# Routing in plain fp32 in four column groups, choosing and placing once per batch

## The reference

```python
h = einsum('bsd,bdh->bsh', x, W[cat]) + b[cat][:, None, :]     # 4 x 1024 x 512
probs = softmax(h.reshape(4096, 512) @ Wr)                     # 4096 x 8
eidx = argmax(probs)                                           # first of the largest
rank = tokens of the same expert before this one               # keep if rank < 512
y[token] = p_tok * (relu(h[token] @ W1[eidx]) @ W2[eidx])      # 512 -> 2048 -> 512
out = x + y
```

## Time and profile before

| | |
|---|---|
| median of 3 runs | 889.83 us (889.78 to 892.02) |
| span of the profiled execution | 890.8 us, mean clock 0.978 |
| TensorE busy | 866.2 us (97%) |
| VectorE, ScalarE, GpSimd busy | 381.9, 253.8, 106.8 us |
| DMA | 126.85 MB, 142 GB/s on average |

### The profile page before, as it was taken

How to read it: one execution, slowest core, us unless ns; L and a number is a source line. 1 busy time by engine, 2 the same in 40 slices (tenths; PEclk the granted TensorE clock), 3 DMA queues, 4 the chain that set the end, 5 groups by cost and what they waited for, 6 DMA issues and landing times.

```text
span 890.8 us, 10524 instructions
## 1 busy us (share of the span) xinstructions
PE 866.2 (97%) x4072; PEld 702.9 (79%) x4073; DVE 381.9 (43%) x603; ACT 253.8 (28%) x361; POOL 106.8 (12%) x120
## 2 busy tenths in 40 slices
PE   8999998899999999999999999999999999999993
PEld 5777775688888888888888888888888888888882
DVE  4576665333343334333434343434343434343432
ACT  3322220323222322232223222322232223222320
POOL 1000001401030103010301030103010300040001
PEclk9898999899999999999999999999999999999997
DMA  8885773823343334233433352334233522241001
GB/s 294 297 296 188 252 281 144 277 98 109 128 168 115 111 126 175 108 114 122 169 107 115 120 179 104 120 116 179 104 118 118 179 100 94 94 170 60 0 0 47
DMA packets 52857, 126.85 MB, mean 142 GB/s; under 512 B 4409, under 2 KB 4409, under 8 KB 52195
## 3 DMA queue, kind: packets, MB, share of 16 engines
q1 hardware_dynamic: 42674, 93.35, 30.1%
q0 software_dynamic: 9584, 32.16, 9.9%
q10 hardware_dynamic: 576, 1.05, 0.4%
HBM read 110.13 MB, written 25.17 MB: 152 GB/s over the span
## 4 chain that ended last, share of the span: by engine, by line
PE 95%; DMA 2%; issue 0%; DVE 0%; SPq 0%; POOL 0%; ACT 0%; POOLq 0%; DVEq 0%
PE acc_ps L793 39%; PE y_ps L776 39%; PE acc_ps L720 7%; PE tp_ps L720 3%; PE y_ps L651 2%; PE tp_ps L666 2%; PE tp_ps L750 2%; DMA stage<-cond_w 1%; DMA h_rows<-rows 1%; DMA rows<-h_rows,tok_all 0%; PE y_ps L699 0%; PE y_ps L750 0%; PE y_ps L675 0%; POOL out L338 0%; PE acc_ps L729 0%
## 5 line engine op out<-in xcount | busy, mean ns | idle before, releaser
L776 PE MATMUL y_ps<-w_split,xt_split 128*128 128x512 f32 x1536 | 371.6, 392 | 0.0
L793 PE MATMUL acc_ps<-xt_split,w_split 128*128 128x512 f32 x1536 | 367.9, 389 | 1.1 <-issue 1.1
L793 PEld LDWEIGHTS acc_ps<-xt_split,w_split 128*128 128x128 f32 x1536 | 288.3, 188 | 61.1 <-issue 1.3
L776 PEld LDWEIGHTS y_ps<-w_split,xt_split 128*128 128x128 f32 x1536 | 286.0, 188 | 58.6
L615 DVE SCALAR_TENSOR_TENSOR xt_split<-acc_ps,xt_split 128x512 fp32r<-128x512 f32 x128 | 88.5, 692 | 386.2 <-ACT xt_split L434 375.7
L434 ACT ACTIVATE xt_split<-acc_ps 128x512 fp32r<-128x512 f32 x128 | 76.6, 598 | 494.0 <-PE acc_ps L793 474.2
L544 DVE TENSOR_TENSOR w_split<-stage,w_split 128x1024 fp32r<-128x1024 f32 x66 | 81.1, 1230 | 19.6 <-ACT w_split L385 18.1
L550 DVE TENSOR_TENSOR w_split<-stage,w_split 128x1024 fp32r<-128x1024 f32 x66 | 80.9, 1226 | 16.4 <-ACT w_split L391 16.4
L338 POOL DMA_INDIRECT out<-rows,put_all x32 | 31.7, 991 | 350.9 <-DVE rows L635 346.1
L720 PE MATMUL acc_ps<-w_split,xt_split 128*128 128x512 f32 x264 | 70.7, 422 | 1.7 <-DVE w_split L465 1.6
L385 ACT ACTIVATE w_split<-stage 128x1024 fp32r<-128x1024 f32 x66 | 69.4, 1051 | 0.0
(11 more groups left out here) (80 smaller groups left out, 261.7 us busy)
## 6 DMA issues: line engine op xcount, KB each, us to landing
stage<-w SPq DMA_DIRECT2D x64, 1024.0 KB, 5.3
stage<-x_t SPq DMA_DIRECT2D x7, 1024.0 KB, 7.3
h_rows<-rows POOLq DMA_DIRECT2D x7, 1024.0 KB, 7.5
stage<-cond_wt SPq DMA_DIRECT2D x4, 1024.0 KB
stage<-cond_w SPq DMA_DIRECT2D x3, 1024.0 KB
stage<-x_t ACTq DMA_DIRECT2D x4, 256.0 KB, 3.3
stage<-cond_w SPq DMA_DIRECT2D x4, 256.0 KB, 3.2
b_rows<-cond_b SPq DMA_DIRECT2D x4, 256.0 KB, 8.3
```

The lines of the kernel that those rows point to most:

```text
L776: last = nc.tensor.matmul(y_ps[:, s, :], hts[:, j % 2, a, s * P:(s + 1) * P], w2s[:, slot, w, kk, :], start=(j == 0 and (a, w) == (HI, HI) ...
L793: last = nc.tensor.matmul(acc_ps[:, j % 2, :], w1s[:, slot, w, k, jj * P:(jj + 1) * P], xts[:, par, a, k, :], start=(k == 0 and (w, a) == ...
```

## The change

- The logits are made in plain fp32 and from the raw x chunk in `stage`, not from its split. The four blocks of the contraction don't add up in one place: block k writes the 32 partitions 32k to 32k+31 of `turn_ps`, with a weight of 32 columns of which eight hold numbers. The sum over the four comes with the turn to tokens: `by_token` is a matmul of the copied logits with `fold`, a 128x8 matrix of four 8x8 identities.
- The product of matrix and Wr is made in the same two steps: `m_turn` (four fp32 matmuls with 512 moving columns, and four of one column for the bias), ScalarE's `copy_turned`, and `m_sum` (four fp32 matmuls with eight columns). VectorE's `copy_m` copies it without a split.
- choose, exps, rank_of, place and fill_table run once for a batch, over eight token tiles.
- The splits of x are two instructions of two blocks each, but for chunk 0.
- SyncE's loads wait for the route that reads the raw chunk (`s_lt`) beside its split, and for `s_turn` in the place of `s_m`.
- The lists of tiles are new. ScalarE's order within a tile is split_xt, split_cond, copy_turned, copy_logits, exps; TensorE's is cond_tile, fill_table, m_turn, m_sum, route, by_token, rank_of.

```diff
-    ROUTE = [3, 5, 7, 9] + [TPC * (c - 1) for c in range(4, NCH)]
-    CHOOSE = [n + 1 for n in ROUTE]
-    PLACE = [n + 2 for n in ROUTE]
-    FILL = [n + 4 for n in ROUTE]
-    PRODUCT = [ROUTE[CPB * b] - (2 if b > 1 else 1) for b in range(BATCH)]
-
-    SPLIT_X = [None, (1, 1, 2, 2), (4, 4, 5, 5), (6, 6, 7, 7)] + [range(TPC * (c - 2), TPC * (c - 1)) for c in range(4, NCH)]
-    SPLIT_W = [None, (4, 5, 6, 6)] + [tuple(2 * TPC * (b - 1) + n for n in (1, 3, 3, 4)) for b in range(2, BATCH)]
+    TPB = TPC * CPB
+    G = 32
+
+    M_TURN = [1, 7, 13, 19]
+    M_SUM = [2, 8, 14, 20]
+    ROUTE = [3, 4, 9, 10, 15, 17, 22, 24]
+    CHOOSE = [5, 11, 18, 25]
+    PLACE = [6, 13, 20, 27]
+    FILL = [8, 15, 22, 29]
+
+    SPLIT_X = [None, (1, 2), (5, 6), (7, 8), (11, 13), (12, 14), (17, 18), (19, 21)]
+    SPLIT_W = [None, (4, 5, 6, 6)] + [tuple(2 * TPC * (b - 1) + n for n in (1, 3, 3, 5)) for b in range(2, BATCH)]
...
             for b in range(1, BATCH):
-                sp.wait_ge(s_xlo, DK * (CPB * b - 1))
+                sp.wait_ge(s_xlo, 2 * (CPB * b - 1) + DK - 2)
+                sp.wait_ge(s_lt, CPB * b - 1)
                 load_xt(CPB * b)
                 sp.wait_ge(s_wlo, DK * b)
                 sp.dma_start(stage[:, 1, :, :], cond_view(b)).then_inc(s_stage[1], 16)
-                sp.wait_ge(s_m, b)
+                sp.wait_ge(s_turn, b)
                 load_cond_wt(b)
-                sp.wait_ge(s_xlo, DK * CPB * b)
+                sp.wait_ge(s_xlo, 2 * CPB * b + DK - 2)
+                sp.wait_ge(s_lt, CPB * b)
                 load_xt(CPB * b + 1)
                 load_bias_rows(b)
                 copy_x(b)
...
+            def copy_turned(b):
+                act.wait_ge(s_turn, b + 1)
+                if b >= 1:
+                    act.wait_ge(s_lg, b)
+                nc.scalar.activation(logits_t[:, 1, :], turn_ps, ACTF.Copy).then_inc(s_turnc, 1)
+
             def copy_logits(c):
-                act.wait_ge(s_msplit, c // CPB + 1)
+                act.wait_ge(s_mcopy, c // CPB + 1)
                 act.wait_ge(s_lt, c + 1)
-                if c >= 2:
-                    act.wait_ge(s_lg, c - 1)
-                nc.scalar.activation(logits_t[:, c % 2, :], tp_ps[0:16, 0, :], ACTF.Identity,
-                                     bias=bias16[:, (c // CPB) % 2:(c // CPB) % 2 + 1]).then_inc(s_ltc, 1)
+                nc.scalar.activation(logits_t[:, c % 2, :], turn_ps, ACTF.Identity,
+                                     bias=bias_g[:, (c // CPB) % 2:(c // CPB) % 2 + 1]).then_inc(s_ltc, 1)
...
+            then(nc.vector.memset(fold[:, :], 0.0))
+            dve.wait_ge(s_mask, 12)
+            for g in range(DK):
+                last = nc.vector.tensor_copy(fold[g * G:g * G + E, :], ident[g * G:g * G + E, g * G:g * G + E])
+            last.then_inc(s_fold, 1)
...
-            def m_product(b):
+            def m_turn(b):
 
                 pe.wait_ge(s_stage[0], 16 * (b + 1))
                 if b == 0:
                     pe.wait_ge(s_const, 16 * (BATCH + 1))
+                    pe.wait_ge(s_wr0, 2)
                 else:
-                    pe.wait_ge(s_msplit, b)
+                    pe.wait_ge(s_ltc, CPB * b)
+                    pe.wait_ge(s_mcopy, b)
+                for k in range(DK):
+                    nc.tensor.matmul(turn_ps[k * G:(k + 1) * G, :], wr32[:, k, :], stage[:, 0, k, :],
+                                     start=True, stop=True)
+                for k in range(DK):
+                    last = nc.tensor.matmul(bias_ps[k * G:(k + 1) * G, :], wr32[:, k, :], b_col[:, b, k:k + 1],
+                                            start=True, stop=True)
+                last.then_inc(s_turn, 1)
+
+            def m_sum(b):
+
+                pe.wait_ge(s_turnc, b + 1)
+                if b == 0:
+                    pe.wait_ge(s_fold, 1)
                 for m in range(DK):
-                    for k in range(DK):
-                        nc.tensor.matmul(m_ps[:, m, :], stage[:, 0, k, m * P:(m + 1) * P], wr16[:, k, 0:E],
-                                         start=(k == 0), stop=(k == DK - 1))
-                for k in range(DK):
-                    last = nc.tensor.matmul(bias_ps, wr16[:, k, :], b_col[:, b, k:k + 1],
-                                            start=(k == 0), stop=(k == DK - 1))
+                    last = nc.tensor.matmul(m_ps[:, m, :], logits_t[:, 1, m * P:(m + 1) * P], fold[:, :],
+                                            start=True, stop=True)
                 last.then_inc(s_m, 1)
 
             def route(c):
 
-                pe.wait_ge(s_msplit, c // CPB + 1)
-                pe.wait_ge(s_xlo, DK * (c + 1))
+                pe.wait_ge(s_mcopy, c // CPB + 1)
                 if c >= 1:
+                    pe.wait_ge(s_stage[2 + c % 2], 16 * ((c + 1) // 2))
+                if c % CPB:
                     pe.wait_ge(s_ltc, c)
                 for k in range(DK):
-                    for part in (HI, LO):
-                        last = nc.tensor.matmul(tp_ps[0:16, 0, :], m_split[:, k, :], xts[:, c % 4, part, k, :],
-                                                start=(k == 0 and part == HI), stop=(k == DK - 1 and part == LO))
+                    last = nc.tensor.matmul(turn_ps[k * G:(k + 1) * G, :], m32[:, (c // CPB) % 2, k, :],
+                                            stage[:, 2 + c % 2, k, :], start=True, stop=True)
                 last.then_inc(s_lt, 1)
 
-            def by_token(c):
+            def by_token(b):
...
+                for t in range(TPB):
+                    last = nc.tensor.matmul(tok_ps[:, t, :], logits_t[:, t // TPC, (t % TPC) * P:(t % TPC + 1) * P],
+                                            fold[:, :], start=True, stop=True)
                 last.then_inc(s_lg, 1)
```

More of the change, by code:

```diff
@@ L402, in _ @@
                 for c in range(1, NCH):
-                    for k in range(DK):
-                        if SPLIT_X[c][k] == n:
-                            split_xt(c, k)
+                    for h in range(2):
+                        if SPLIT_X[c][h] == n:
+                            split_xt(c, h)
                 for b in range(1, BATCH):
@@ L488, in wide @@
             def wide(v):
[L489 to L499, removed]
+                return v.unsqueeze(2).to_broadcast([P, TPB, E])
@@ L500, in choose @@
+            def choose(b):
+                dve.wait_ge(s_lg, b + 1)
+                then(nc.vector.tensor_reduce(top[:, :], tok_ps, AX.X, ALU.max))
+                if b >= 1:
+                    dve.wait_ge(s_exp, b)
                 chained[0] += 1
-                nc.vector.tensor_tensor(diff[:, par, :, :], lg[:, :, :], wide(top[:, :]), ALU.subtract
+                nc.vector.tensor_tensor(diff[:, :, :], tok_ps, wide(top[:, :]), ALU.subtract
                                         ).then_inc(s_diff, 1)
@@ L512, in choose, with place @@
                                         ).then_inc(s_oh, 1)
[L514 to L519, removed]
+            def place(b):
+                tiles = slice(TPB * b, TPB * (b + 1))
+                dve.wait_ge(s_exp, b + 1)
+                then(nc.vector.tensor_reduce(total[:, :], expo[:, :, :], AX.X, ALU.add))
@@ L668, in route @@
                 last.then_inc(s_lt, 1)
-            def by_token(c):
-                pe.wait_ge(s_ltc, c + 1)
-                if c >= 1:
-                    pe.wait_ge(s_oh, c)
-                for t in range(TPC):
-                    last = nc.tensor.transpose(tok_ps[:, t, :], logits_t[:, c % 2, t * P:(t + 1) * P],
-                                               ident[0:16, 0:16])
-                last.then_inc(s_lg, 1)
-            def rank_of(c):
-                pe.wait_ge(s_oh, c + 1)
-                if c >= 1:
-                    pe.wait_ge(s_sel, c)
-                nc.tensor.matmul(rank_ps, before[:, :], onehot[:, c % 2, :, :].rearrange("p t e -> p (t e)"),
+            def by_token(b):
+                pe.wait_ge(s_ltc, CPB * (b + 1))
+                if b >= 1:
+                    pe.wait_ge(s_oh, b)
+                for t in range(TPB):
+                    last = nc.tensor.matmul(tok_ps[:, t, :], logits_t[:, t // TPC, (t % TPC) * P:(t % TPC + 1) * P],
+                                            fold[:, :], start=True, stop=True)
+                last.then_inc(s_lg, 1)
@@ L685, in rank_of @@
+            def rank_of(b):
+                pe.wait_ge(s_oh, b + 1)
+                if b >= 1:
+                    pe.wait_ge(s_sel, b)
+                nc.tensor.matmul(rank_ps, before[:, :], onehot[:, :, :].rearrange("p t e -> p (t e)"),
                                  start=True, stop=False)
-                for t in range(TPC - 1):
-                    later = TPC - 1 - t
+                for t in range(TPB - 1):
+                    later = TPB - 1 - t
                     nc.tensor.matmul(rank_ps[:, (t + 1) * E:], ones[:, :],
-                                     onehot[:, c % 2, t:t + 1, :].to_broadcast([P, later, E]),
```

(13 more changed lines are left out.)

167 lines of the change are left out of this document (90 added, 77 removed).

## The result

| | before | changed |
|---|---|---|
| median | 890.02 us (889.78 to 892.02, 4 runs) | 911.88 us (906.67 to 913.43, 4 runs) |
| span of the profiled execution | 890.8 us | 910.2 us (its time 911.96) |
| start of the expert loop | 164.02 us | 173.81 us |
| expert stage, to the end | 726.8 us | 736.4 us |

The changed kernel is slower: ratio 1.0224, 95% interval 1.0197 to 1.0251 (whether by 2% or more the interval leaves open), against a forecast of +10 us (+1.2%). Of the 19.4 us between the two spans, 9.8 came in the front stage, where the change is, and 9.6 in the expert loop, which it doesn't touch. The prediction had the sign and the range, but not these two halves.

The account below looks back on a forecast made before the run. TensorE, busy in 97% of the span, was taken as the bound; -24.3 + 14.0 + 3.7 + 4.2 + 2.5 + 1.1 + 8.6 + 0.6 = +10.4 us on the median of 889.8 gave 900 us, range 885 to 917.

Parts of the forecast that it names:

- r: Length of a route on TensorE, eight fp32 records in four column groups: 1.0, 2.3 or 3.6 us by overlap; 2.3 taken.
- I take 2.3: two records of one call can't share their group: Routes and m_turn: records start in order, a group's second waits for its first, so 2.3 us each; chance 0.42.
- rival 1: Routes and m_turn: the column groups overlap fully, r = 1.0, giving 887.9 us; chance 0.28.
- The price of one record: One plain fp32 record with 512 columns on TensorE: 0.43 us, from the fp32 transpose of 128 columns.
- The loads: Condition matrices, issued behind routes, hold up ScalarE's copy_logits until about 9.1 us after the route; TensorE waits 1.1 and 6.3.
- the wait of batch 2: TensorE ahead of route(3): one tile of 2.8 us covers 9.1, so a wait of 6.3 us.
- batch 1: TensorE ahead of by_token(0), after tile 5: tile, route, tile cover 7.9 of 9.1 us, wait 1.1.
- batch 3: Condition matrix 3, issued behind route 4 (tile 15), wanted by ScalarE at tile 17: covered, no wait.
- The clock behind waits: TensorE's slow clock after a wait: +2.3 us, priced behind the wait ahead of route(3) only.
- Rival 4: Front stage: the clock also falls behind each by_token, 4 x 1.6 us, 906.6; inside the main forecast's 0.42.
- First wait: TensorE ahead of m_turn(0), behind tile 1: waits for the bias columns until about 18.7 us, +2.5 us.
- The expert loop "isn't touched": Expert loop: the change lies wholly in the front stage, so the loop got no cost of its own.

Follow-up runs that it names:

- e4: Changed kernel with the four blocks of a route and of the bias added up in the first column group: 923.05 us, one run.
- e3: Changed kernel with the next condition matrix's load issued ahead of SyncE's wait for the route: 890.17 us, ratio 0.9984 to the kernel before.
- e9: Changed kernel, loads still late, with splits of the next condition matrices and x chunk 6 moved behind the copy: 898.05 us, ratio 1.0068 to the kernel before.
- e1: Changed kernel with 40 one-column matmuls more on TensorE ahead of the expert loop: 901.08 us, ratio 1.0124 to the kernel before.

## Why the prediction was right, and where it was not

The number held (911.9 in 885 to 917, slower at 0.72) and the point was 12 us low, by two errors that took each other away and one cost that it didn't have. That the number held is luck in good part. TensorE's own new work was forecast 17 us too dear, the waits and the clock behind them 19 us too cheap (sums of the rows above against the prediction's terms), and the expert loop added 9.6. By its own signs the prediction was wrong: it named r under 1.2 as one, and r is 0.99, a case in which it expected 887.9 us and a kernel that is not slower.

- **The step "I take 2.3: two records of one call can't share their group" failed.** r is 0.99, rival 1's value, which had 0.28. Records of different groups start together, so no pair blocks the next. It made 12 uses 1.3 us too dear, 15.7 us (most of the 17). The price of one record, 0.43 from the fp32 transpose, was right: 0.44 in e4. The rule of the Trainium skill, "TensorE: Matmul & The Clock Gate", Part 3, that groups start together agrees with these rows; the one that matmuls start in program order, by which I chose, would give 2.3 and doesn't, unless the eight reach the array in another order than they were called in, which no run here tells.
- **The loads: mechanism right, size too small.** That copy_logits would stand behind split_cond, and where, was forecast; the wait of batch 2 was 6.84 (6.3; the prediction's 7.7 + 0.62 + 0.68 is 9.0 and not 9.1, which changes nothing). But the landing was taken as 7.2 from a pair with less in the queues (a DMA share of 0.72, where it was 1.05 and 1.02 during the first two waits here). It was 7.7 to 11.0, so batch 1 waited 5.47 and not the 2.4 that go with r = 1.0, and batch 3, which I called covered, 3.34. Its cover, from the end of route 4 to `by_token(2)`, was 9.7 us, and the copy ended 13.0 us after route 4. e3 and e9 show the mechanism, from both ends.
- **The clock behind waits** was priced once, at 2.3, and came four times, 11.9 us; behind the very wait for which it was priced it was 1.9. Rival 4, the clock falling behind `by_token` by itself, is wrong: at full clock it left the next tile at full clock.
- **First wait** 2.62 (2.5), `m_sum` and `by_token` 0.85 and 1.70 (0.9 and 1.75), last store 0.7 late (0.6), no loss in place, choose and `fold`: as forecast. The row of the first wait names `cond_wt`, but that load was issued at 7.88 us and took 9.5, so it was there at 17.4; the last bias columns, issued at 11.8, took at least 6.6 us and came at 18.4 at the earliest, so it is they, as the prediction has it.
- **The expert loop "isn't touched"** failed as a step: its code isn't, but its place in TensorE's instruction stream is. 9.6 us, not in any rival. The Trainium skill, "Runtime: NRT & Kernel Launch", Instruction fetch mechanics, has TensorE hold 2,048 instructions, refilled in blocks of 16 KB or 256 instructions, and has a taken branch wait for a fetch when its target isn't in "the current 2-page window". The packets of 16 KB and the waits at the loop's turns agree with the blocks and the fetch. The window of two pages does not: a turn of the loop is some 1,670 instructions by estimate (800 matmul records in the trace, as many weight loads, and the waits), over six blocks, and in e1 it turns without a fetch. Had I counted the loop against the 2,048, its place would have been a rival.
- The forecast, which knew nothing of this last cost, was 900 for r = 2.3 and 888 for r = 1.0; e1, the change without that cost, is at 901. So the front stage ended by luck where the forecast for r = 2.3 had it, with a route less than half as dear and waits twice as dear.

## What to carry to other kernels

A load that must wait for one more reader also holds back every load behind it in the queue, and an engine that waits for such a load holds back every small copy behind it: list, for each moved release, what stands behind it on the issuing queue and on the consumer, and price the landing with what else is in flight, not by the best pair. Price a wait of TensorE with the half clock behind it: in the front stage here waits of 1.8 to 6.8 us were followed by losses of 1.6 to 4.3 us, the longest wait not by the largest. In the expert loop, where TensorE runs without gaps, the waits of 1.6 and 2.4 us were followed by 0.1, and the one of 2.2 by 1.7. When a kernel ends in a long hardware loop, look at the instruction queue's packets after any edit ahead of it, since adding or removing a few instructions can move the time by 1% either way.

## What the hardware showed that I had not expected

- Four plain fp32 matmuls of 128x512 with 32-column weights, eight records, took 0.99 us in four column groups and 3.56 in one.
- The loop over pairs of experts stood 1.6 to 2.7 us at each turn, or not at all, depending on 40 one-column matmuls ahead of it: 40 packets of instructions against 13, and 9.6 us.
